# Routed expert blocks: the outer product from split operands in three passes, with its splits on ScalarE and VectorE

## The reference, cut to what matters

```python
E = 16; K = 2; DIM = 512; INTER = 128
def step(y, p):
    w1, b1, w2, b2, w3, b3, ge = p
    h = jax.nn.silu(xt @ w1 + b1) * (xt @ w2 + b2)
    return (y + ge[:, None] * (h @ w3 + b3), None)
y, _ = jax.lax.scan(step, jnp.zeros_like(xt), (ew1, eb1, ew2, eb2, ew3, eb3, gate.T))
```

## Time and profile before

| | |
|---|---|
| median of 3 runs | 1226.1 us (1225.43 to 1226.37) |
| the profiled execution | 1224.71 us, its span 1223.0 us |
| granted TensorE clock, mean | 0.986 of full speed |
| instructions | 20618 |
| TensorE, VectorE, ScalarE, GpSimd busy | 96%, 68%, 48%, 29% of the span |

### The profile page before, as it was taken

One profiled execution on the slowest core, in us unless ns is written; L12 is line 12 of the kernel. 1 busy time (PEld: TensorE's weight loads), 2 busy tenths in 40 slices (PEclk: granted clock), 3 DMA queues, 4 the chain that ended last, 5 costly groups with the idle time before them and its releaser, 6 DMA issues.

```text
span 1223.0 us, 20618 instructions
## 1 busy us (share of the span) xinstructions
PE 1169.9 (96%) x6956; PEld 1005.2 (82%) x6956; DVE 832.4 (68%) x2373; ACT 588.2 (48%) x1364; POOL 348.8 (29%) x302
## 2 busy tenths in 40 slices
PE   7899999999999999999999999998999999899992
PEld 6798888988889888889888888887887777578871
DVE  6767667666676666676676776669788878784334
ACT  4545455454545545555454545445444455524441
POOL 5313022221312312132130321203343312445661
PEclk8999999999999999999999999999999999999996
DMA  7011000000101100010010000001212323833435
GB/s 275 1 36 52 2 35 18 35 34 0 51 0 34 31 20 34 0 51 0 34 51 0 34 0 1 1 1 54 83 55 74 106 69 103 321 126 126 144 103 206
DMA packets 37465, 73.57 MB, mean 60 GB/s; under 512 B 6098, under 2 KB 22482, under 8 KB 35366
## 3 DMA queue, kind: packets, MB, share of 16 engines
q1 hardware_dynamic: 30726, 56.38, 13.3%
q0 software_dynamic: 4960, 12.33, 3.2%
q10 hardware_dynamic: 1728, 4.20, 0.9%
HBM read 64.50 MB, written 12.32 MB: 63 GB/s over the span
## 4 chain that ended last, share of the span: by engine, by line
PE 59%; DVE 21%; issue 9%; ACT 5%; POOL 2%; DMA 2%; SPq 1%; DVEq 0%; ACTq 0%; POOLq 0%
PE bank L354 14%; PE bank L356 14%; PE bank L355 14%; PE bank L1978 5%; PE bank L1847 3%; DVE probs L1159 3%; ACT probs L790 3%; PE bank L1688 2%; PE bank L1989 2%; DVE k_junk L1116 2%; DVE iq L1322 2%; DVE row_max L1132 2%; DVE pt_lo L1146 2%; POOL k_rstd L577 1%; PE bank L1630 1%
## 5 line engine op out<-in xcount | busy, mean ns | idle before, releaser
L790 ACT ACTIVATE probs<-bank,exp_bias,q_rstd 128x256 f32<-128x256 f32 x256 | 141.3, 562 | 138.0 <-DVE exp_bias L1140 138.0
L1151 DVE TENSOR_TENSOR o_lo<-bank,o_hi 128x512 fp32r<-128x512 f32 x64 | 44.3, 692 | 178.6 <-ACT o_hi L783 178.6
L354 PE MATMUL bank<-wkv_hi,kv_src_lo 128*128 128x256 f32 x512 | 145.8, 285 | 1.4 <-DVE kv_src_lo L1184 1.4
L355 PE MATMUL bank<-wkv_lo,kv_src_hi 128*128 128x256 f32 x512 | 145.6, 284 | 0.0
L356 PE MATMUL bank<-wkv_hi,kv_src_hi 128*128 128x256 f32 x512 | 145.5, 284 | 0.0
L581 POOL TENSOR_TENSOR q_rstd<-q_var,minus_half 128x8 f32<-128x8 f32 x32 | 52.7, 1646 | 300.4 <-DVE q_var L1119 300.4
L779 ACT ACTIVATE pt_hi<-bank 128x512 fp32r<-128x512 f32 x128 | 69.6, 596 | 116.2 <-PE bank L1688 116.2
L354 PE MATMUL bank<-wo_hi,o_lo 128*128 128x512 f32 x256 | 104.2, 407 | 1.7 <-DVE o_lo L1151 1.2
L577 POOL TENSOR_TENSOR k_rstd<-k_var,minus_half 128x4 f32<-128x4 f32 x32 | 32.5, 1016 | 249.1 <-DVE k_var L1093 249.1
L354 PE MATMUL bank<-wq_hi,kv_src_lo 128*128 128x512 f32 x256 | 102.8, 401 | 0.8 <-POOL wq_lo L566 0.8
L356 PE MATMUL bank<-wo_hi,o_hi 128*128 128x512 f32 x256 | 101.5, 397 | 0.0
(11 more groups left out here) (257 smaller groups left out, 3090.6 us busy)
## 6 DMA issues: line engine op xcount, KB each, us to landing
weights<-r_w SPq DMA_DIRECT2D x16, 768.0 KB, 9.3
wq_raw<-wq SPq DMA_DIRECT2D x8, 1024.0 KB, 4.7
wo_raw<-wo SPq DMA_DIRECT2D x8, 1024.0 KB, 4.8
wkv_raw<-wkv SPq DMA_DIRECT2D x8, 512.0 KB, 3.3
gu_raw<-w_gate SPq DMA_DIRECT2D x10, 256.0 KB, 3.4
gu_raw<-w_up SPq DMA_DIRECT2D x10, 256.0 KB, 3.8
wd_raw<-w_down SPq DMA_DIRECT2D x10, 256.0 KB, 4.1
x_sb<-x SPq DMA_DIRECT2D x4, 512.0 KB, 9.8
```

The costliest lines, as they stand in the source:

```text
L354: eng.matmul(out_ap, a_lo, b_hi, start=start, stop=False)
L355: eng.matmul(out_ap, a_hi, b_lo, start=False, stop=False)
L790: act.activation(probs[:, h, :], scores_ps[h // 2][:, (h % 2) * 256:(h % 2) * 256 + 256], ACT.Exp, bias=exp_bias[:, h:h + 1], scale=q_rstd ...
L1151: dve.tensor_tensor(o_lo[:, par, :], o_ps[:, :], o_hi[:, par, :].bitcast(F32), ALU.subtract)\
```

## The change

The outer product of a routed block is no longer one f32 matmul from `weights`, but three passes of split operands. ScalarE makes the high parts: `w3_hi` (512 columns of the expert's outer weights, after a load of the offset) and `g_hi`. VectorE makes the low parts `w3_lo` (after a load of the offset of its own) and `g_lo`. The hidden rows are now called `g_h`. TensorE's own offset loads go. `w3_hi` and `w3_lo` lie where the shared experts' outer weights `e3_hi` and `e3_lo` lay, so the first of them wait for the last shared product. Some semaphores are merged (`bias_step`, `sel_step`) with the same waits.

```diff
+            def inner_rows_high(j):
+                act.wait_ge(g_h_ready, j + 1)
+                if j >= 2:
+                    act.wait_ge(r_done, j - 1)
+                act.activation(g_hi[:, j % 2, :], g_h[:, j % 2, :], ACT.Copy).then_inc(g_hi_ready, 1)
+
+            def outer_weights_high(j):
+                if j >= 2:
+                    act.wait_ge(r_done, j - 1)
+                else:
+                    act.wait_ge(e_done, NB)
+                    act.wait_ge(offset_ready, 1)
+                    act.wait_ge(weights_loaded, 16 * E)
+                at_w = act.value_load(offset_i[0:1, j:j + 1], min_val=0, max_val=(E - 1) * EW)
+                act.activation(w3_hi[:, j % 2, :], weights[:, bass.ds(at_w + 2 * D, D)], ACT.Copy).then_inc(w3_hi_ready, 1)
...
+            outer_weights_high(0)
+            outer_weights_high(1)
             take_x_cols(0)
             take_x_cols(1)
             routed_silu(0)
+            inner_rows_high(0)
             for j in range(TILES):
                 if j + 1 < TILES:
                     routed_silu(j + 1)
                 if j + 2 < TILES:
                     take_x_cols(j + 2)
+                if j + 1 < TILES:
+                    inner_rows_high(j + 1)
                 take_y(j)
+                if j + 2 < TILES:
+                    outer_weights_high(j + 2)
...
             def routed_hidden(j):
                 dve.wait_ge(g_silu_ready, j + 1)
                 if j >= 2:
-                    dve.wait_ge(r_done, j - 1)
-                dve.scalar_tensor_tensor(out=g_ht[:, j % 2, :], in0=bank[j % 2][:, P:2 * P], scalar=block_b[:, 1, j:j + 1],
-                                         in1=g_silu[:, j % 2, :], op0=ALU.add, op1=ALU.mult).then_inc(g_ht_ready, 1)
+                    dve.wait_ge(g_hi_ready, j - 1)
+                    dve.wait_ge(g_ht_ready, j - 1)
+                dve.scalar_tensor_tensor(out=g_h[:, j % 2, :], in0=bank[j % 2][:, P:2 * P], scalar=block_b[:, 1, j:j + 1],
+                                         in1=g_silu[:, j % 2, :], op0=ALU.add, op1=ALU.mult).then_inc(g_h_ready, 1)
+
+            def inner_rows_low(j):
+                dve.wait_ge(g_hi_ready, j + 1)
+                dve.tensor_tensor(g_lo[:, j % 2, :], g_h[:, j % 2, :], g_hi[:, j % 2, :].bitcast(F32), ALU.subtract)\
+                    .then_inc(g_ht_ready, 1)
+
+            def outer_weights_low(j):
+                dve.wait_ge(w3_hi_ready, j + 1)
+                at_w = dve.value_load(offset_i[0:1, j:j + 1], min_val=0, max_val=(E - 1) * EW)
+                dve.tensor_tensor(w3_lo[:, j % 2, :], weights[:, bass.ds(at_w + 2 * D, D)], w3_hi[:, j % 2, :].bitcast(F32),
+                                  ALU.subtract).then_inc(w3_lo_ready, 1)
...
+            outer_weights_low(0)
+            outer_weights_low(1)
             for j in range(TILES):
                 routed_hidden(j)
                 if j + 2 < TILES:
                     take_weights(j + 2)
+                inner_rows_low(j)
+                if 2 <= j + 1 < TILES:
+                    outer_weights_low(j + 1)
...
-                pe.matmul(bank[6 + j % 2][:, :], g_ht[:, j % 2, :], weights[:, bass.ds(at_weights[j] + 2 * D, D)],
-                          start=True, stop=True).then_inc(r_done, 1)
+                pe.wait_ge(w3_lo_ready, j + 1)
+                three(pe, bank[6 + j % 2][:, :], g_hi[:, j % 2, :], g_lo[:, j % 2, :], w3_hi[:, j % 2, :],
+                      w3_lo[:, j % 2, :], True, True).then_inc(r_done, 1)
...
-            for j in range(4):
-                load_offset(j)
-            pe.wait_ge(weights_loaded, 16 * E)
...
-                if j + 4 < TILES:
-                    load_offset(j + 4)
```

More of the change, by code:

```diff
@@ L213, in build @@
         e12_lo = put("e12_lo", [P, 2, 2 * KC, P], F32R)
+        here = at[0]
         e3_hi = put("e3_hi", [P, 2, D], F32R)
         e3_lo = put("e3_lo", [P, 2, D], F32R)
+        at[0] = here
+        w3_hi = put("w3_hi", [P, 2, D], F32R)
+        w3_lo = put("w3_lo", [P, 2, D], F32R)
         e_h_at = at[0]
@@ L242, in build @@
         g_silu = put("g_silu", [P, 2, P])
-        g_ht = put("g_ht", [P, 2, P])
+        g_h = put("g_h", [P, 2, P])
+        g_hi = put("g_hi", [P, 2, P], F32R)
+        g_lo = put("g_lo", [P, 2, P], F32R)
         bank = [top.enter_context(nc.psum_tensor(f"bank{i}", [P, 512], F32)) for i in range(8)]
@@ L295, in build @@
         weights_loaded = sem("weights_loaded")
-        bias_zeroed, bias_high, bias_split = (sem(n) for n in ("bias_zeroed", "bias_high", "bias_split"))
+        bias_step = sem("bias_step")
         rows_stored = [sem(f"rows_stored{i}") for i in range(2)]
         maps_ready = sem("maps_ready")
-        chosen_ready, ranks_done, sel_ready, sel_turned = (sem(n) for n in ("chosen_ready", "ranks_done", "sel_ready", "sel_turned"))
-        sel_copied, offset_ready = sem("sel_copied"), sem("offset_ready")
+        chosen_ready, ranks_done, sel_step = (sem(n) for n in ("chosen_ready", "ranks_done", "sel_step"))
+        offset_ready = sem("offset_ready")
         places_ready, tokens_done, tokens_ready = sem("places_ready"), sem("tokens_done"), sem("tokens_ready")
@@ L463, in _ @@
                 sp.dma_start(dst, src).then_inc(moe_small_loaded, 16)
-            sp.wait_ge(bias_zeroed, 1)
+            sp.wait_ge(bias_step, 1)
             for row in (0, 32, 64):
@@ L941, in _ @@
             act.activation(router_wh[:, :, :], router_wr[:, :, :], ACT.Copy).then_inc(router_w_hi, 1)
-            act.activation(bias_t[:, :], bias_raw[:, :], ACT.Copy).then_inc(bias_high, 1)
+            act.activation(bias_t[:, :], bias_raw[:, :], ACT.Copy).then_inc(bias_step, 1)
             def down_whole(t):
@@ L1022, in routed_silu @@
                 if j >= 2:
-                    act.wait_ge(g_ht_ready, j - 1)
+                    act.wait_ge(g_h_ready, j - 1)
                 else:
@@ L1497, in take_selection @@
             def take_selection():
-                dve.wait_ge(sel_turned, 1)
-                dve.tensor_copy(sel_t[:, :], bank[7][:, 0:TL + 2]).then_inc(sel_copied, 1)
+                dve.wait_ge(sel_step, 3)
+                dve.tensor_copy(sel_t[:, :], bank[7][:, 0:TL + 2]).then_inc(sel_step, 1)
             def take_tokens():
@@ L1940, in turn_selection @@
             def turn_selection():
-                pe.wait_ge(sel_ready, 2)
+                pe.wait_ge(sel_step, 2)
                 pe.transpose(bank[7][:, 0:TL + 2], sel[0:TL + 2, :], ident[0:TL + 2, 0:TL + 2])\
-                    .then_inc(sel_turned, 1)
+                    .then_inc(sel_step, 1)
             def gather_tokens():
-                pe.wait_ge(sel_copied, 1)
+                pe.wait_ge(sel_step, 4)
                 for c in range(TOP):
@@ L2042, in _ @@
             pe.wait_ge(logits_ready, 2)
-            pe.wait_ge(bias_split, 1)
+            pe.wait_ge(bias_step, 3)
             rank_tokens()
```

17 lines of the change are left out of this document (7 added, 10 removed).

## The result

The changed kernel takes 1233.07 us (median of 8 runs, 1231.38 to 1234.81) against 1226.57 of the kernel before, timed beside it (8 runs): ratio 1.0050, interval 1.0037 to 1.0064, so 6.5 us slower where 2.8 was forecast. Timed once more on another chip it gave 1.0049 (1.0036 to 1.0062). Both are slower by more than the 0.2% that can be told.

A forecast was written before the change was run, and what follows sets the result against it. The prediction took the loop of turns, `x_cols` copy and inner product (3.17 us a block) as the bound. Product 0, start +1.7, end +0.6, late blocks +0.5 gave +2.8 us: 1228.9 us, range 1226.8 to 1235.5.

The forecast's parts named there:

- +1.7: Start of the routed loop: first outer product 1.9 us late, less 0.18 for being shorter.
- +0.6: End of the routed loop: last inner product's end to last outer result, 2.84 us in place of 2.21.
- step that named VectorE's queue: Start: two `w3_lo`, 0.60 us apart, go ahead of `g_h(0)` on VectorE, so it runs at 1105.53.
- +0.5 for blocks in which 0.02 of slack doesn't cover a late instruction: Routed loop: allowance of 0.5 us, a choice, for late blocks, with the split loop 3.15 us against 3.17.
- loop of `w3_hi`, `w3_lo`, `g_h` and `g_hi`: Steady block: new closed loop between ScalarE and VectorE, 3.15 us against the block's 3.17, so barely hidden.
- TensorE's has the same 0.30 as VectorE's, so I take 0.70 there too: ScalarE's offset load ahead of `w3_hi`: 0.70 us with register work, bounds 0.57 and 1.0.
- so 0.67 are left and x_cols isn't touched: Steady block: `w3_hi` ends at 2.70 us on ScalarE, its next silu is due at 3.37.
- rival (b): Routed loop: the ScalarE and VectorE loop exceeds 3.17 us and becomes the bound; 1231.3 to 1236.5 us; 27%.
- sign of (b): Routed loop: period above 3.25 us with TensorE's turns or product waiting on `g_lo`, silu or `y_rows`.
- (d): Routed loop: the outer product is the limit after all, up to 5.2 us won, less 2.3; 1223.2 us; 8%.
- (e): Routed loop: GpSimd's indirect issues hold up `w3_lo`, half a microsecond more per block; about 1242 us; 5%.
- (c): Whole kernel: cheaper than summed, late blocks vanish and the end costs 0.2 less; 1227.7 us, down to 1226.8; 15%.

The follow-up runs named there:

- e1: The kernel before, with each routed block's outer product on 128 of its 512 weight columns; 1225.86 us, ratio 0.9993.
- e2: The changed kernel with one of the three passes (high times high) alone; 1230.75 us, ratio 1.0038.
- e10: The changed kernel with ScalarE's offset load at the head of the block's turn and `gate_slots` behind the block loop; 1229.02 us, ratio 1.0026.
- e7: The changed kernel with ScalarE's offset loads removed, `w3_hi` taken from constant addresses; 1227.96 us, ratio 1.0032.
- e3: The changed kernel with four buffers for `w3_hi` and `w3_lo`, and `w3_hi` made three blocks ahead; 1231.40 us, ratio 1.0043.
- e6: The changed kernel with weight slices split for blocks 0 and 1 only, all other blocks reusing them; 1227.12 us, ratio 1.0019.
- e8: The kernel before, with `gate_slots` moved behind the block loop; 1224.97 us, ratio 1.0003.
- e4: The kernel before, with turns of block j+2 ahead of the inner product of j+1 and `x_cols` ahead of silu; 1230.19 us, ratio 1.0038.
- e11: The kernel before, with turns ahead as in e4, six gather buffers in place of four and `gate_slots` behind the loop; 1222.00 us, ratio 0.9967.
- e9: The changed kernel with ScalarE's offset load at the head of the block's turn, ahead of its wait for the inner product; 1232.12 us, ratio 1.0055.
- e12: The changed kernel with gathers of blocks 4 to 31 as plain transfers from SyncE, not GpSimd's indirect ones; 1229.11 us, ratio 1.0034.
- e5: The changed kernel once more, with no edit; 1231.11 us, ratio 1.0049.

## Why the prediction was right, and where it was short

**Right: the bound.** The change was called free of gain because the inner product waits for `x_cols` and not for the outer product. e1 and e2 show it from both kernels: three quarters of the product taken away gave 0, two of three passes nothing in the loop. That TensorE's offset loads go gave nothing in the loop either, as written (3.17 stays 3.17).

**Right: start and end.** +1.7 and +0.6 were summed. The table has 11.47 against 9.84 and 5.40 against 4.79. The step that named VectorE's queue, with two `w3_lo` ahead of `g_h(0)`, as the place is shown by e10, where moving other work out of that queue removed all of it.

**Mis-sized: the ScalarE load, and with it "+0.5 for blocks in which 0.02 of slack doesn't cover a late instruction".** The loop of `w3_hi`, `w3_lo`, `g_h` and `g_hi` was written out as 3.15. Measured piece by piece on quiet blocks it is 3.10: `w3_lo` starts 0.77 after `w3_hi` ends (0.74 written), `g_h` 0.61 later (0.60), `g_hi` 0.37 later (0.39), and `w3_hi` 0.72 after that (0.80). The slack was 0.07, not 0.02. But "TensorE's has the same 0.30 as VectorE's, so I take 0.70 there too" failed: ScalarE's load takes 0.28 to 0.55, in 15 of the 19 blocks 3 to 21 over 0.39. In the prediction's term, load and register work, that is 0.63 to 0.90 in place of 0.70, and the loop is 3.24 to 3.38 where it is slow. With it fell the walk's "so 0.67 are left and x_cols isn't touched": the slack is used up, `w3_hi` reaches silu's moment and delays `x_cols` through it. This is rival (b) with its price of a slow load, but only over the stretch of blocks in which loads are slow, and only once the start's lead of some blocks is used up. It cost 1.8 us (blocks 9 to 21). e7 shows that it is the load, e3 that it acts through the loop. The prediction's own sign of (b), a period above 3.25, was there in part: eight of blocks 10 to 20 took 3.25 to 3.38, though TensorE waited for `x_cols`, behind the late silu.

**Not foreseen: the stops.** The prediction had seen two of 0.3 to 0.4 (they are 0.42 and 0.43) in the kernel before and took them as they were. By difference, some 2.5 us of the changed kernel are neither start, late blocks nor end, and most likely they are larger stops. Large ones were seen only with ScalarE's per-block offset load: in before, e1, e6, e7 and e8, which lack it, no block behind the third is over 0.43 late (in e4 and e11, whose loop is another one, single blocks are up to 0.8 late), while in the changed kernel, e2, e3, e9 and e10 single blocks lose 1.0 to 1.5, often at a multiple of four. The load isn't needed for small ones: the kernel before is late at blocks 20 and 28, e1 by 0.08 to 0.15 at 12, 16, 20, 24 and 28. So something recurs every fourth block in both kernels, and it is the size that goes with the loads. No large stop is in the profile of e12 either, which keeps the loads and takes the gathers from GpSimd; but one profile without stops proves little, as e5, with no edit, has none over 0.40. In the two shown ScalarE is late with nothing on record ahead of it that is. The mechanism stays open: neither the instruction fetches in the trace (16 KB about every 14 to 21 us, 8 KB every 8 to 20) nor the clock (1.00 throughout) fall together with them.

**Rivals that fell.** (d): no pass is on the loop's path. (e): `w3_lo` took 0.69 in every block from the second on, beside indirect issues or not, and what it was built on, 1675 ns in the mean at L1322, has another cause: these operations are slow only beside GpSimd's own two-input operations (the last section). One `w3_lo` in all runs was slow, the first of e10, the only one made while GpSimd did its own additions. (c), 1.6 above before, was not reached by any variant that keeps the three passes: even e6, with no stop, no late block and only start and end left, is 2.6 above, about the sum's 2.8.

The 6.5 us, then: 1.6 start, 1.8 late blocks, each shown by an edit that takes it away; 0.6 end, of which e6 takes a part and e2 all; and a remainder of 2.5 us, of which e6 takes some 2.0 and e7 some 1.4, most likely stops, whose mechanism is not shown. That the measured time lies within 1226.8 to 1235.5 is owed in part to luck: of the 3.7 us above the forecast 2.8, only 1.3 (1.8 for the 0.5 summed) came by a path that was written down, the rest by one that no rival had.

## What to carry to other kernels

When TensorE looks full, look at one block for the wait that ends last: two limits that coincide make a shorter product worth nothing, until the other loop is opened (e11). Write out the new loop that a split across two engines closes, and if its slack is 2%, price every instruction in it on its own engine and beside the traffic that it will meet, for a scalar loaded from SBUF is quick or slow by turns. Work that was harmless in a queue at the start of a loop stops being so when new work must come behind it (`gate_slots`: 0 before, 1.6 us after).

## What the runs showed of the hardware

- A load of 4 bytes of SBUF into a ScalarE register took 0.28 us at best and up to 0.56 (0.81 once, in e12), nearly the same for the same block in repeated executions of a kernel. After the last scatter with rows (that of block 18) it was always quick, before that mostly slow. The same load on VectorE, at another moment of the block, took 0.30 nearly always.
- silu and `x_cols` on ScalarE sometimes start 0.1 to 1.5 us after TensorE's recorded work and their own queue would let them, mostly at blocks that are multiples of four; in e9 at five in a row, by 1.03 to 1.06 us at four of them.
- An indirect gather of 256 KB, beside a scatter, took 3.3 to 4.6 us from the start of its issue to the turns that were waiting for it (e4: 23 waits, 19.4 us). Four buffers sound like four blocks, some 12 us, of lead, but each issue stands in GpSimd's queue behind a scatter that waits for `y_rows`: in the kernel before it began 5.0 to 5.7 us ahead of its turns in the loop, with six buffers (e11) 8.5 to 10.4, and TensorE waited for none of them (1110 to 1195).
- VectorE was held up by GpSimd where both read two operands from SBUF. In e10 the first `w3_lo` was made while GpSimd still added shared rows, and took 2.04 us where all 30 others took 0.68 to 0.69:

```profile
1099.92 2.48 POOL L690 TENSOR_TENSOR x_sb<-s_rows,x_sb 128x512 f32<-128x512 f32 x2
1100.91 2.64 DVE L1585 TENSOR_TENSOR w_lo<-weights,w_hi 128x512 fp32r<-128x512 f32 x2 [0.76 <-ACT w_hi L1056]
...
1102.56 1.23 POOL L714 DMA_INDIRECT x_rows<-rows_dram,token_i  x1 [0.16 <-issue]
```

  The kernel before has it eight times, ahead of the routed blocks. Of its 22 operations at L1322, 14 have no GpSimd operation beside them and take 0.69; the eight that overlap one of GpSimd's splits take 2.21 to 2.77. One of each kind, and the split beside the second:

```profile
906.49 0.69 DVE L1322 TENSOR_TENSOR iq<-tr_int,tr_sign 128x512 f32 x1
910.67 2.62 POOL L625 TENSOR_TENSOR gu_lo<-gu_raw,gu_hi 128x1024 fp32r<-128x1024 f32 x1 [7.19 <-ACT gu_hi L867]
...
911.18 2.66 DVE L1322 TENSOR_TENSOR iq<-tr_int,tr_sign 128x512 f32 x1
```

  Both slow ones shown end 0.55 us after a GpSimd operation has ended (1102.40 and 1102.95; 913.29 and 913.84). The Trainium skill (SBUF — State Buffer, "SBUF: two separate sides") describes an exclusive lock between a VectorE operation with two SBUF inputs and a GpSimd operation that reads SBUF, and these pairs agree with it. GpSimd's indirect issues, beside which `w3_lo` kept its 0.69, don't act like that.
